# Cross-attention: other places for three kinds of transposes within an item, and two more scores ahead of the stage

## The chip, the cores and the metric

The kernel runs on one core of a Trainium2 chip. The metric is the device time of one execution in microseconds (us). The engines are named as in the profile: PE is TensorE, PEld its weight loads, DVE VectorE, ACT ScalarE, POOL GpSimd; SP issues most of the transfers.

## The reference

One decoder layer over x of 4 x 512 x 512, float32, in three parts, each added to x:

```
x = x + self_attention(layernorm(x))          # 16 heads of 128, causal, grouped keys
x = x + cross_attention(layernorm(x), ctx)    # 32 query heads of 16, 8 key heads of 16
x = x + ffn(layernorm(x))                     # 8 experts of 352, two for each token, one shared of 704

# cross-attention: q = layernorm(x), k = v = ctx (4 x 512 x 128), no projections
scores  = einsum('bkgsd,bktd->bkgst', qh, kh) / sqrt(16)
weights = softmax(scores)
out     = einsum('bkgst,bktd->bkgsd', weights, vh)
```

The change lies in the cross-attention.

## The kernel before, in words

The program is written engine by engine. Each engine runs its own instruction list in order, and waits on counters (semaphores) of the others. The three parts of the layer follow one another; the cross-attention lies between about 876 and 1265 us of the span.

**Items and steps.** The cross-attention is cut into 32 items (`ITEMS`): batch `m // 8` and key head `m % 8` of item `m`, with four query heads each. An item has 16 scores of 128x512 for the row maxima (`score`, line 1188), 16 transposed scores (line 1308) that ACT exponentiates (line 1560), and the product of the exponentials with the values (the results, line 1318). `cross_steps(m)` writes the order: eight steps `k` of 0 to 7, and in each: a score, two transposed scores, a score, perhaps a turn, and in the odd steps a quarter of the results of the item before (four matmuls of 32 columns side by side, one for each query head). PE, DVE and ACT all walk this one list, each taking the operations that are its own.

**The two kinds of scores.** A score goes to one of three PSUM banks, and DVE takes its row maximum out (`maximum`, line 1767); so the score `u` waits for the maximum of `u - 3`. The maxima of an item are subtracted inside the transposed scores, as two more rows of the queries (50 rows instead of 48). They must therefore be known before the item begins. So the scores run ahead of the items: `S_FIRST` of them are made in the tail of the self-attention (`START_CHAINS`, `START_END`, `START_MID`), and within item `m` the list makes scores `S_FIRST + 16 m` and following. A transposed score also has three banks, emptied by ACT's exponential.

**The turns.** A turn is a transpose on PE through one shared PSUM bank, `XT`. There are three kinds in an item, placed by `turns_in(m, k)`:

- the maxima turn `("m", m + 1)`: POOL splits the 16 maxima into a high and a low part (lines 996, 999), PE turns them (one matmul, line 196), ACT copies them out (line 1512), and SP moves them to DRAM and back into the rows of the queries (lines 780, 784);
- the raw turn: normalized queries `("q", ...)` in most even items, or the keys of a coming batch `("k", ...)` in items 1, 9 and 17: four matmuls, a copy of ACT (line 1516), a split by POOL (lines 947, 949), and transfers by SP (lines 736 to 772);
- the result turn `("o", m - 2)`: four matmuls that turn the results of item `m - 2`, which ACT copied out of PSUM at the end of item `m - 1` (line 1566). DVE then takes a reciprocal (line 1924) and at once divides (line 1906), and POOL adds to `res` (line 1007). Within DVE's list the reciprocal and the division stand behind the two maxima of the same step.

Each turn waits until the turn before it has been taken out of `XT`.

**Other work of DVE.** `norm_piece(b, kv, k)` puts the layer norms of the next batches at the ends of steps: the statistics of one tile (line 207), a group of small operations, or one normalized query tile (line 1752). Which items have one, and in which step, hangs on `m % 8` and the batch.

Of the kernel before, what the change touches and what calls it, by code (L numbers as in the profile page):

```python
# [68 lines left out]

FIRST_TURNS = [("k", 0), ("q", 0), ("q", 1), ("m", 0)]  # L70

S_FIRST = 30

START_CHAINS = {(2, 6): [("moments",)], (2, 8): [("roots",)], (3, 1): [("queries",)]}
START_END = {(3, 1): [("first_t", "k", 0)], (3, 2): [("first_t", "q", 0)], (3, 4): [("first_t", "q", 1)],
             (3, 14): [("first_t", "m", 0)]}
for at, us in ((6, (0, 1)), (7, (2, 3)), (8, (4, 5)), (10, (10, 11)), (11, (12, 13)), (12, (14, 15)), (18, (24, 25)),
               (19, (26, 27)), (20, (28, 29))):
    START_END[3, at] = [("first_s", u) for u in us]
for at, us in ((9, (6, 7)), (13, (16, 17)), (17, (20, 21))):  # L80
    START_CHAINS[3, at] = [("first_s", u) for u in us]
# [150 lines left out]
KV, XG, XD = 8, 4, 16  # L232
# [7 lines left out]
ITEMS = BATCH * KV  # L240
S_UNITS = XG * TOK_TILES
VW = 32


def turns_in(m, k):

    if k == 2 and m + 1 < ITEMS:
        return [("m", m + 1)]
    if k == 4 and m % 2 == 0 and m + 4 < ITEMS:
        return [("q", m // 2 + 2)]  # L250
    if k == 4 and m % KV == 1 and m + KV < ITEMS:
        return [("k", m // KV + 1)]
    if k == 6 and m >= 2:
        return [("o", m - 2)]
    return []


def cross_steps(m):


    ops = []
    for k in range(8):
        at = S_FIRST + S_UNITS * m + 2 * k
        units = [("s", n) for n in (at, at + 1) if n < S_UNITS * ITEMS]
        ops += units[0:1]
        if m < ITEMS:

            ops += [("st", 2 * k + 1), ("st", 2 * k)]
        ops += units[1:]
        ops += [("t",) + turn for turn in turns_in(m, k)]  # L270
        if 1 <= m <= ITEMS and k % 2:
            ops.append(("pv", k // 2))
        ops.append(("end", k))
    return ops

# [137 lines left out]
def mixed_tile(n):  # L413

    return n // 4 * 2 + n % 2, n // 2 % 2
# [8 lines left out]
def build(nc, x, ctx_in, w_qkv_t, w_proj_t, gate_t, w1_t, w2_t, w3_t, kinds, out):  # L424
# [11 lines left out]
    with ExitStack() as whole:  # L436
# [271 lines left out]
        def _(sp):  # L708
# [38 lines left out]
            def keep_queries(a):  # L747
                if a >= 2:
                    for n in (2 * a - 4, 2 * a - 3):
                        sp.wait_ge(s_xq3[n % 4], 32 * (n // 4 + 1))  # L750
                to_rows(q_way[a % 2], q_hi, q_lo, s_xqh, s_xql, a + 1, s_xqs)
# [100 lines left out]
            for m in range(ITEMS):  # L852
                if m + 1 < ITEMS:
                    move_maxima(m + 1)
                if m + 3 < ITEMS:
                    take_queries(m + 3)
                if m % KV == KV // 2 and m + KV < ITEMS:
                    take_keys(m // KV + 1, 0)
                if m % KV == 0 and m:
                    take_keys(m // KV, 1)  # L860
                for kind, n in turns_in(m, 4):
                    if kind == "q":
                        keep_queries(n)
                    else:
                        keep_keys(n)
                        if n + 1 < BATCH:
                            context(n + 1)
                for q in (2 * (m - KV - 1), 2 * (m - KV - 1) + 1):
                    if 0 <= q < N_ROUTED:
                        blank(q)  # L870
                if m >= ITEMS - 2:
                    load_piece(m - (ITEMS - 2), 0)
# [44 lines left out]
        def _(pool):  # L917
# [100 lines left out]
            def cross(m):  # L1018
# [11 lines left out]
                    clear_values(1)  # L1030
                if kv == 0 and b + 1 < BATCH:
                    order_keys(b + 1)
                for kind, n in turns_in(m, 4):
                    if kind == "q":
                        split_queries(n)
                    else:
                        split_keys(n)
                        build_values(n)
# [8 lines left out]
            for m in range(ITEMS + 2):  # L1047
                cross(m)
# [37 lines left out]
            for n in range(TOP * TILES):  # L1086
                t, r = mixed_tile(n)
# [8 lines left out]
        def _(pe):  # L1096
# [181 lines left out]
            def cross(m):  # L1278
                for op in cross_steps(m):
# [16 lines left out]
                    elif op[0] == "s":  # L1296
                        u = op[1]
                        pe.wait_ge(s_xmax, max(S_FIRST, u - 2))
                        score(u, XS + u % 3)
# [847 lines left out]
```

## Time and profile before

| | |
|---|---|
| time, median of 3 runs | 1773.65 us (1769.39 to 1777.32) |
| the profiled execution: own time | 1780.01 us |
| its span (first to last instruction) | 1778.1 us |
| mean granted clock of TensorE | 0.967 |
| PE busy | 1700.2 us, 96% of the span |
| DVE busy | 1213.6 us, 68% |
| ACT busy | 921.6 us, 52% |
| POOL busy | 182.8 us, 10% |

The busy shares are means over the three parts of the layer. The self-attention and the last part keep PE near full; in the cross-attention DVE has 16 maxima of 128x512 in each item beside its other work, and PE, DVE and ACT hand PSUM banks to one another every few hundred nanoseconds. A busy PE isn't PE at its peak, since matmuls overlap and their ends are modelled. What is read from a row below is thus the start of an instruction and the idle time before it.

### The profile page before, as it was taken

Reading aid. Unit: us, or ns where it says so; the run is one execution under the profiler, and the core shown is the slowest. Engines: PE = TensorE matmul, PEld = TensorE weight load, DVE = VectorE, ACT = ScalarE, POOL = GpSimd, SP = SyncE. Lnnn points to the kernel's source line nnn. Section 1 sums busy time; section 2 is a strip of 40 time slices with the busy share of each in tenths; the row PEclk is TensorE's granted clock in tenths of the full one; section 3 lists DMA queues with packets and bytes.
Section 4 is the critical chain, followed back from the end, with each engine's and each line's share of the span. In section 5 each row is a group of like instructions: output and inputs, shape, how many; then the busy total and the mean of one; then the engine's idle time right before and its main releaser. Section 6 shows DMA issues by size and latency. Waiting matters only on the chain.

```text
span 1778.1 us, 26288 instructions
## 1 busy us (share of the span) xinstructions
PE 1700.2 (96%) x9497; PEld 1303.7 (73%) x9497; DVE 1213.6 (68%) x2733; ACT 921.6 (52%) x1937; POOL 182.8 (10%) x297
## 2 busy tenths in 40 slices
PE   5799999999999999989899999999899999999998
PEld 4688888888888888876533333333699999999997
DVE  6666666666666666676589999997434267676766
ACT  2444445445444444442378887877431146666641
POOL 1000000000000000011122323221105100000024
PEclk9899999999999999997699999999799999999999
DMA  4000100010000000004023544442103178787846
GB/s 154 1 1 7 30 1 25 1 36 1 25 1 15 23 24 1 1 20 110 28 72 92 151 140 156 129 131 81 59 1 137 66 264 285 271 298 266 297 134 229
DMA packets 103203, 167.20 MB, mean 94 GB/s; under 512 B 8324, under 2 KB 52356, under 8 KB 102308
## 3 DMA queue, kind: packets, MB, share of 16 engines
q1 hardware_dynamic: 97956, 148.74, 25.9%
q0 software_dynamic: 5120, 16.78, 2.8%
q8 instruction: 77, 1.26, 0.3%
q14 instruction: 50, 0.41, 0.1%
HBM read 116.15 MB, written 49.28 MB: 93 GB/s over the span
## 4 chain that ended last, share of the span: by engine, by line
PE 84%; DVE 11%; ACT 3%; issue 1%; DMA 1%; POOL 0%; SPq 0%; DVEq 0%; ACTq 0%
PE ps L190 44%; PE ps L196 9%; PE ps L1433 8%; PE ps L1236 7%; PE ps L1318 6%; PE ps L1188 6%; DVE xmax L1767 4%; PE ps L1308 3%; DVE al L1782 1%; ACT ah L1538 1%; DVE stats L207 1%; PE ps L1369 1%; DVE ptl L1774 1%; DVE probs L1733 1%; ACT xp L1560 1%
## 5 line engine op out<-in xcount | busy, mean ns | idle before, releaser
L1767 DVE TENSOR_REDUCE xmax<-ps 128x1 f32<-128x512 f32 x512 | 319.1, 681 | 24.4 <-PE ps L1188 24.3
L1560 ACT ACTIVATE xp<-ps 128x512 f32<-128x512 f32 x512 | 273.5, 601 | 96.0 <-PE ps L1308 95.6
L1493 ACT ACTIVATE probs<-probs,nmax 128x128 f32<-128x128 f32 (+3 forms) x256 | 144.1, 563 | 160.7 <-DVE nmax L1733 160.7
L1188 PE MATMUL ps<-k,q 48*128 48x512 f32 x512 | 212.1, 487 | 8.0 <-DVE xmax L1767 5.1
L1308 PE MATMUL ps<-q,k 50*128 50x512 f32 x512 | 198.8, 472 | 6.1 <-ACT xp L1560 6.0
L1188 PEld LDWEIGHTS ps<-k,q 48*128 48x128 f32 x512 | 87.7, 192 | 147.4 <-DVE xmax L1767 113.0
L1533 ACT CAST pth<-ps 128x128 fp32r<-128x128 f32 (+3 forms) x256 | 107.0, 418 | 85.9 <-PE ps L196 85.9
L1318 PE MATMUL ps<-xp,vx 128*32 128x512 f32 x1024 | 140.1, 621 | 0.8 <-issue 0.8
L1733 DVE CUSTOM_DVE_ANT_0 probs<-ps,mask 128x128 f32<-128x128 f32 (+3 forms) x256 | 123.4, 482 | 10.0 <-PE ps L190 9.8
L1774 DVE TENSOR_TENSOR ptl<-ps,pth 128x128 fp32r<-128x128 f32 (+3 forms) x256 | 123.8, 484 | 2.0 <-ACT pth L1533 2.0
L196 PE MATMUL ps<-ident,probs 128*128 128x128 f32 x640 | 113.1, 275 | 8.7 <-DVE ptl L1774 6.6
L190 PE MATMUL ps<-w12h,x_h 128*128 128x352 f32 x568 | 121.1, 335 | 0.0
L1782 DVE TENSOR_TENSOR al<-ps,ah 128x512 fp32r<-128x512 f32 x64 | 44.2, 691 | 107.1 <-ACT ah L1538 107.1
L190 PE MATMUL ps<-w12h,x_l 128*128 128x352 f32 x568 | 116.0, 327 | 0.0
L190 PE MATMUL ps<-w12l,x_h 128*128 128x352 f32 x568 | 115.6, 326 | 0.0
L190 PE MATMUL ps<-xh,wh 128*128 128x512 f32 x384 | 111.7, 414 | 2.1 <-DVE wl L1711 2.1
L1949 DVE TENSOR_TENSOR w12l<-w_raw,w12h 128x1408 fp32r<-128x1408 f32 x56 | 90.7, 1620 | 27.9 <-ACT w12h L1591 27.9
L1308 PEld LDWEIGHTS ps<-q,k 50*128 50x128 f32 x512 | 81.8, 191 | 33.4 <-ACT xp L1560 26.7
L1742 DVE TENSOR_SCALAR probs<-probs,rinv 128x128 f32<-128x128 f32 (+3 forms) x256 | 99.8, 390 | 9.1
L1538 ACT CAST ah<-ps 128x512 fp32r<-128x512 f32 x64 | 37.6, 587 | 131.5 <-PE ps L1236 131.5
L196 PEld LDWEIGHTS ps<-ident,probs 128*128 128x128 f32 x640 | 81.7, 141 | 32.4 <-DVE probs L1742 10.3
L190 PE MATMUL ps<-xh,wl 128*128 128x512 f32 x384 | 105.3, 396 | 0.0
(188 smaller groups left out, 3553.6 us busy)
## 6 DMA issues: line engine op xcount, KB each, us to landing
w_raw<-in_w_t SPq DMA_DIRECT2D x56, 704.0 KB, 5.9
w_raw<-in_w_t SPq DMA_DIRECT2D x28, 768.0 KB, 5.8
q<-q_way SPq DMA_DIRECT2D x64, 192.0 KB, 3.2
rows_x<-w_raw SPq DMA_DIRECT2D x39, 256.0 KB, 3.4
mixed<-rows_x SPq DMA_DIRECT2D x39, 256.0 KB, 4.4
rows_y<-y_s SPq DMA_DIRECT2D x39, 256.0 KB, 5.4
q_way<-q_hi SPq DMA_DIRECT2D x32, 256.0 KB, 3.6
w_raw<-in_w_qkv_t SPq DMA_DIRECT2D x24, 256.0 KB, 3.0
```

The lines of the kernel that those rows point to most:

```text
L190: last = pe.matmul(dst, lhs, rhs, start=(n == 0), stop=(n == len(pairs) - 1))
L196: return pe.matmul(dst, src, ident, start=True, stop=True, is_transpose=True)
L1188: pe.matmul(ps[:, bank, :], q3[rows, m % 4, h // 2, i * P:(i + 1) * P].bitcast(F32R), k3[rows, m % KV, :].bitcast(F32R), start=True, stop= ...
L1236: pv = pe.matmul(ps[:, O_BANK + h % 2, j * P:], v[:, b % 2, j, :], p[:, 4 * j:3 * j + TOK_TILES, :].rearrange("p i n -> p (i n)"), start=( ...
L1308: pe.matmul(ps[:, XST + n % 3, :], k3[rows, m % KV, t * P:(t + 1) * P].bitcast(F32R), q3[rows, m % 4, h // 2, :].bitcast(F32R), start=True ...
L1318: ins = pe.matmul(ps[VW * h:VW * (h + 1), XO, :], vx[:, n // KV % 2, n % KV, j, :], xp[:, n % 2, h, j, :], start=(j == 0), stop=(j == TOK_ ...
L1433: ins = pe.matmul(ps[:, HY + n % 2, :], lhs, rhs, start=(step.opens and m == 0), stop=(step.closes and m == len(pairs) - 1))
L1493: act.activation(probs[u % 4][:, 0:w], probs[u % 4][:, 0:w], ACT.Exp, scale=-1.0, bias=nmax[:, u % 4:u % 4 + 1], accum_out=rsum[:, u % 4:u ...
L1560: act.activation(xp[:, m % 2, h, t, :], ps[:, XST + n % 3, :], ACT.Exp, scale=X_SCALE).then_inc(s_xe, 1)
L1733: dve.tensor_tensor_reduce(probs[u % 4][:, 0:w], ps[:, S_BANK + u % 2, 0:w], mask[:, SEQ - w:], -1.0, LARGEST, ALU.add, ALU.min, nmax[:, u ...
L1767: dve.tensor_reduce(xmax[:, m % 2, h % 2, h // 2, i:i + 1], ps[:, bank, :], AX_X, ALU.max, negate=True).then_inc(s_xmax, 1)
L1774: dve.tensor_tensor(ptl[:, i:4 * i + 1:3, :], ps[:, T_BANK + (1 + t) % 2, 0:(i + 1) * P].rearrange("p (j n) -> p j n", n=P), pth[:, i:4 * ...
```

## The change

`MAXIMA_AT, RAW_AT, RESULT_AT = 1, 5, 7` takes the place of the steps 2, 4 and 6 of the three kinds of turns. In these odd steps a quarter of the results follows as well: the raw turn and the result turn stand ahead of it, the maxima turn behind it. DVE's reciprocal and division move with the result turn, from the end of step 6 to the end of step 7. `S_FIRST` grows from 30 to 32: scores 30 and 31 go to the last step of the self-attention, and every item makes scores that are two further ahead. SP's and POOL's lists read `RAW_AT` where they read 4 before; their own order is unchanged.

```diff
-S_FIRST = 30
+S_FIRST = 32
...
-               (19, (26, 27)), (20, (28, 29))):
+               (19, (26, 27)), (20, (28, 29, 30, 31))):
...
+MAXIMA_AT, RAW_AT, RESULT_AT = 1, 5, 7
+
+
 def turns_in(m, k):
 
-    if k == 2 and m + 1 < ITEMS:
+    if k == MAXIMA_AT and m + 1 < ITEMS:
         return [("m", m + 1)]
-    if k == 4 and m % 2 == 0 and m + 4 < ITEMS:
+    if k == RAW_AT and m % 2 == 0 and m + 4 < ITEMS:
         return [("q", m // 2 + 2)]
-    if k == 4 and m % KV == 1 and m + KV < ITEMS:
+    if k == RAW_AT and m % KV == 1 and m + KV < ITEMS:
         return [("k", m // KV + 1)]
-    if k == 6 and m >= 2:
+    if k == RESULT_AT and m >= 2:
         return [("o", m - 2)]
...
-        ops += [("t",) + turn for turn in turns_in(m, k)]
+        ops += [("t",) + turn for turn in turns_in(m, k) if k != MAXIMA_AT]
         if 1 <= m <= ITEMS and k % 2:
             ops.append(("pv", k // 2))
+        ops += [("t",) + turn for turn in turns_in(m, k) if k == MAXIMA_AT]
```

**PE's list, the maxima turn.** L1188 (L1192 in the change) is a score for a maximum, L1308 (L1312) a transposed score, L1318 (L1322) a quarter of the results, `xm` the split maxima. Before, from step 1 of an item on:

```order
L1188 MATMUL ps<-k,q 128x512
L1318 MATMUL ps<-xp,vx 32x512 x4
L1188 MATMUL ps<-k,q 128x512
L1308 MATMUL ps<-q,k 128x512 x2
L1188 MATMUL ps<-k,q 128x512
L196 MATMUL ps<-ident,xm 32x128
```

Now, from the same place on:

```order
L1192 MATMUL ps<-k,q 128x512
L1322 MATMUL ps<-xp,vx 32x512 x4
L196 MATMUL ps<-ident,xm 32x128
L1192 MATMUL ps<-k,q 128x512
L1312 MATMUL ps<-q,k 128x512 x2
```

The turn of the maxima now stands between the results and the next score, where nothing stood.

**PE's list, the raw turn and the result turn of an even item.** `xn` are the normalized queries, `o_t` the results of item `m - 2`. Before, from step 4 on; the last quarter of the results follows the last row:

```order
L196 MATMUL ps<-ident,xn 128x128 x4
L1188 MATMUL ps<-k,q 128x512
L1308 MATMUL ps<-q,k 128x512 x2
L1188 MATMUL ps<-k,q 128x512
L1318 MATMUL ps<-xp,vx 32x512 x4
L1188 MATMUL ps<-k,q 128x512
L1308 MATMUL ps<-q,k 128x512 x2
L1188 MATMUL ps<-k,q 128x512
L196 MATMUL ps<-ident,o_t 128x128 x4
L1188 MATMUL ps<-k,q 128x512
L1308 MATMUL ps<-q,k 128x512 x2
L1188 MATMUL ps<-k,q 128x512
```

Now, from step 5 on:

```order
L196 MATMUL ps<-ident,xn 128x128 x4
L1322 MATMUL ps<-xp,vx 32x512 x4
L1192 MATMUL ps<-k,q 128x512
L1312 MATMUL ps<-q,k 128x512 x2
L1192 MATMUL ps<-k,q 128x512 x2
L1312 MATMUL ps<-q,k 128x512 x2
L1192 MATMUL ps<-k,q 128x512
L196 MATMUL ps<-ident,o_t 128x128 x4
L1322 MATMUL ps<-xp,vx 32x512 x4
L1192 MATMUL ps<-k,q 128x512
```

Both turns now stand between the last score of an odd step and its results; before, each had two scores and two transposed scores between itself and the next results.

**DVE's list, the reciprocal and the division.** L1767 (L1771) is a maximum, L207 a layer norm's statistics of one tile. Before, from the last maxima ahead of step 4 of an item on:

```order
L207 BN_STATS stats<-res 128x6
L1767 TENSOR_REDUCE xmax<-ps 128x1 x6
L1924 RECIPROCAL xrec<-ps 128x16
L1906 TENSOR_TENSOR xo<-ps,xrec 128x256
L1767 TENSOR_REDUCE xmax<-ps 128x1 x10
```

Now:

```order
L207 BN_STATS stats<-res 128x6
L1771 TENSOR_REDUCE xmax<-ps 128x1 x8
L1928 RECIPROCAL xrec<-ps 128x16
L1910 TENSOR_TENSOR xo<-ps,xrec 128x256
L1771 TENSOR_REDUCE xmax<-ps 128x1 x8
```

The division stands behind all 16 maxima of the item, where it stood ahead of the last two.

## Rows read from the trace of the kernel before

**Rows 1.** Groups of instructions, 930 to 1180 us: busy us, mean ns | idle before it.
```profile
L1767 DVE TENSOR_REDUCE xmax<-ps 128x1 f32<-128x512 f32 x348 | 216.1, 681 | 11.7 <-PE ps L1188 11.7
```

**Rows 2.** Windows of 50 us, busy us by engine, granted clock, DMA share, GB/s.
```profile
930.00:980.00 50.00, 49.32 (x311) 19.17 (x310) 47.89 (x84) 40.41 (x82) 11.03 (x18) 1.00 0.31 83
```

**Rows 3.** Timeline of DVE, item 6: start us, us, instructions [idle before <-releaser].
```profile
953.12 2.48 DVE L1767 TENSOR_REDUCE xmax<-ps 128x1 f32<-128x512 f32 x4 [0.22 <-PE ps L1188]
955.52 0.68 DVE L207 BATCH_NORM_STATS2 stats<-res 128x6 f32<-128x512 f32 x1
956.12 2.47 DVE L1767 TENSOR_REDUCE xmax<-ps 128x1 f32<-128x512 f32 x4
958.81 1.29 DVE L1767 TENSOR_REDUCE xmax<-ps 128x1 f32<-128x512 f32 x2 [0.22 <-PE ps L1188]
960.01 0.25 DVE L1924 RECIPROCAL xrec<-ps 128x16 f32<-128x16 f32 x1
...
960.64 3.67 DVE L1767 TENSOR_REDUCE xmax<-ps 128x1 f32<-128x512 f32 x6
```

**Rows 4.** Timeline of PE, item 6.
```profile
951.16 0.50 PE L1188 MATMUL ps<-k,q 48*128 48x512 f32 x1
...
951.59 1.06 PE L1318 MATMUL ps<-xp,vx 128*32 128x512 f32 x8
...
952.58 0.50 PE L1188 MATMUL ps<-k,q 48*128 48x512 f32 x1
...
953.25 0.28 PE L196 MATMUL ps<-ident,xm 128*32 128x128 f32 x1
...
953.47 0.49 PE L1188 MATMUL ps<-k,q 48*128 48x512 f32 x1
...
953.86 0.49 PE L1188 MATMUL ps<-k,q 48*128 48x512 f32 x1
...
955.94 0.66 PE L196 MATMUL ps<-ident,xn 128*128 128x128 f32 x4
...
956.53 0.50 PE L1188 MATMUL ps<-k,q 48*128 48x512 f32 x1
```

**Rows 5.** Timeline of DVE, item 22: an even item without statistics.
```profile
1138.45 2.48 DVE L1767 TENSOR_REDUCE xmax<-ps 128x1 f32<-128x512 f32 x4 [0.21 <-PE ps L1188]
1141.14 2.54 DVE L1767 TENSOR_REDUCE xmax<-ps 128x1 f32<-128x512 f32 x4 [0.21 <-PE ps L1188]
1144.07 1.29 DVE L1767 TENSOR_REDUCE xmax<-ps 128x1 f32<-128x512 f32 x2 [0.39 <-PE ps L1188]
```

**Rows 6.** Timeline of DVE, item 26: statistics in every odd step.
```profile
1184.14 2.47 DVE L1767 TENSOR_REDUCE xmax<-ps 128x1 f32<-128x512 f32 x4
1186.52 0.68 DVE L207 BATCH_NORM_STATS2 stats<-res 128x6 f32<-128x512 f32 x1
```

**Rows 7.** Timeline of PE, the last results of the stage: a result turn ahead of results.
```profile
1259.96 0.66 PE L196 MATMUL ps<-ident,o_t 128*128 128x128 f32 x4
...
1260.55 1.07 PE L1318 MATMUL ps<-xp,vx 128*32 128x512 f32 x8
```

**Rows 8.** Timeline, the start of the cross-attention.
```profile
874.54 1.28 DVE L1767 TENSOR_REDUCE xmax<-ps 128x1 f32<-128x512 f32 x2
...
875.97 0.47 PE L1188 MATMUL ps<-k,q 48*128 48x512 f32 x1 [1.64 <-DVE xmax L1767]
...
876.47 2.48 DVE L1767 TENSOR_REDUCE xmax<-ps 128x1 f32<-128x512 f32 x4 [0.65 <-PE ps L1188]
```

**Rows 9.** Timeline of PE, item 30, which has next to no scores.
```profile
1239.67 0.66 PE L196 MATMUL ps<-ident,o_t 128*128 128x128 f32 x4
...
1240.86 1.06 PE L1318 MATMUL ps<-xp,vx 128*32 128x512 f32 x8
```

**Rows 10.** Window of 2 us in item 1, columns as in rows 2.
```profile
894.00:896.00 2.00, 2.00 (x12) 0.26 (x10) 1.50 (x3) 1.25 (x4) 0.00 (x0) 0.50 0.03 8
```

**Rows 11.** DMA issues: KB each, us to landing.
```profile
q<-q_way SPq DMA_DIRECT2D x64, 192.0 KB, 3.2
```

More of the change, by code:

```diff
@@ L860, in _ @@
                     take_keys(m // KV, 1)
-                for kind, n in turns_in(m, 4):
+                for kind, n in turns_in(m, RAW_AT):
                     if kind == "q":
@@ L1032, in cross @@
                     order_keys(b + 1)
-                for kind, n in turns_in(m, 4):
+                for kind, n in turns_in(m, RAW_AT):
                     if kind == "q":
```

## The prediction

> **What bounds the kernel now.** I read the groups of instructions first, then the windows, and then the timelines of DVE and PE over one item, since the change touches the cross-attention alone. There 348 maxima take DVE 216.1 us of a stretch of 250 us, and the only idle time ahead of them is 11.7 us, all of it waiting for a score from PE [rows 1]. The window shows both engines close to full, DVE 47.89 and PE 49.32 of 50 us, at a granted clock of 1.00, which is the level of 2.4 GHz [rows 2]. 348 maxima are 21.75 items, so an item takes 11.5 us. The stage runs at DVE's pace plus what PE makes it wait, with a few tenths of slack on either engine in each item. The order inside an item decides who waits.
>
> Where does DVE wait? Four maxima on end take 2.40 us, 0.60 each: 953.12 to 955.52. The next four, from 956.12 to 958.81, take 2.69 [rows 3]. So 0.29 us are lost there, and the row says PE. I rebuild that loss from PE's starts, since all that follows is made in the same way. Call the start of the first score of an even step 0. Its maximum begins at 0.54 (952.58 to 953.12) [rows 3, 4] and ends 0.68 later [rows 1], at 1.22. That frees the bank for the last score of the odd step, which starts at 1.28 (952.58 to 953.86). Its results follow 0.43 later (951.16 to 951.59) and hold PE for 0.99 (951.59 to 952.58) [rows 4]. So the next step's first score starts at 2.70, and its maximum can start at 3.24. DVE, with four maxima, is free at 0.54 + 2.40 = 2.94. The difference, 0.30, is the 0.29 of the row. **Every odd step thus has a window that PE overruns by 0.29 us, unless DVE has other work in it.** Where it has, nothing is lost: with a tile's statistics between the maxima the next four follow without idle time [rows 3, 6]. The reciprocal and the division, 0.63 together (960.01 to 960.64) [rows 3], stand after the 14th maximum and lie in the window of step 7: the six maxima behind them run on without a stop.
>
> **The change, part by part.** No operation is added or removed. Four things move. At full clock there are items 2 to 29; they have a window at each odd step.
>
> *Raw turn, step 4 to step 5.* Four transposes hold PE for 0.59 (955.94 to 956.53) [rows 4]. In an even step they cost little: where no statistics stand ahead, the window of step 5 loses 0.53 instead of 0.29 (1141.14 to 1144.07 is 2.93) [rows 5]. Where statistics do, it loses the plain 0.29 of rows 3. Now the turn stands between the last score and the results: 1.28 + 0.43 + 0.59 + 0.99 + 0.54 = 3.83 against 2.94, a loss of 0.89. Items 4, 6, 12 and 14 have statistics in step 3: 4 x 0.60. Eight other even items and the two key turns of items 9 and 17: 10 x 0.36. Item 26 has statistics in step 5 too, of 0.60: 0.29. Sum **6.3 us**.
>
> *Result turn, step 6 to step 7.* It holds PE for the same 0.59, and nothing hides under results that follow: at the stage's end the results start 0.59 after such a turn (1259.96 to 1260.55) [rows 7]. The window of step 7 is then 3.83 on PE. On DVE it keeps the division, now behind its last maximum: 2.94 + 0.63 = 3.57. The loss is 0.26 where it was none. It goes where DVE has a query tile or statistics in that window as well (items 2, 10, 18, 26, 27, 28); 22 items are left: **5.7 us**.
>
> *Maxima turn, step 2 to behind the results of step 1.* It holds PE for 0.22 (953.25 to 953.47) [rows 4]. In step 2 that was hidden, since an even step has time to spare. Now it makes the window of step 1 lose 0.51 instead of 0.29, in the 13 items where DVE has no layer norm work at the ends of steps 0 and 1 (5 to 8, 13 to 16, 21 to 25): **2.9 us**. It could cost 0 (it hides) or 0.33 (with 0.11 us of lead that PE loses to the later result turn); I take the turn's own row. Its consumers gain: the maxima go out to DRAM and back a step earlier.
>
> On the maxima turn the Trainium skill has a rule that would make it cheaper. TensorE: Matmul & The Clock Gate, section "Part 3: Packing small matmuls", says that matmuls on different column strips of the array run at the same time. The turn has 32 columns, as each of the four results matmuls does, so by that rule it would run beside the last of them and the 2.9 us would be about 0.
>
> *Two more scores ahead.* Before, PE waits 1.64 us at the stage's start for maximum 29, and DVE then 0.65 for score 30 (876.47) [rows 8]. Now score 30 goes as soon as maximum 28 is out, at 874.54 + 0.68 = 875.22; maxima 30 and 31 follow at about 875.8 and 876.4; score 32 waits for all 32, until 877.1, and its maximum comes at 877.6. Before, it came at 876.47 + 2 x 0.60 = 877.67. DVE gains nothing; the gap moves. But the items begin 1.1 us later, and item 30 has one more step without scores to do after the last maximum: **1.2 us** lost.
>
> *The end.* Items 30 and 31 have next to no scores, and PE and ACT wait for one another there. In item 30 the result turn has two transposed scores between itself and the results (1239.67 to 1240.86) [rows 9], so ACT has work while PE turns. In step 7 it stands straight ahead of the results: 0.59, plus 0.22 for the item's maxima turn: **0.8 us**. For item 31 I count nothing; its bound is the same 0.6. Item 1 runs at half clock as well (0.50, 1.2 GHz) [rows 10]; PE is busy for all of that row while DVE has 1.50 of 2.00, so a turn costs the same wherever it stands: I take **0.3 us** for the maxima turn.
>
> Sum: 6.3 + 5.7 + 2.9 + 1.2 + 0.8 + 0.3 = **17.2 us** slower. The profiled execution took 1780.0 and would take 1797.2; it stands 6.4 above the median of the runs, 1773.65. I forecast from that median: **1791 us**. The lower bound of the sum has every turn hidden: 10 x 0.24 of today's raw turns are won, 1.2 is lost at the start, -1.2 in all. The upper has each turn pay in full and DVE's other work cover nothing: 14 x 0.6 + 22 x 0.59 + 13 x 0.33 + 2.3 = 28.
>
> **The rivals.**
>
> 1. *Covered turns* (not slower). PE catches up within each window because its 0.43 between score and results is slack, and the turns fit there or run beside the results. Place: steps 1, 5 and 7. Price: the lower bound, 1772.5 us. It decides if the loop's extra cost is under 0.25 us an item (28 x 0.25 = 7, plus the 2.3 of start and end, is the half per cent). For it: two matmuls of different row halves do overlap on PE. Against it: the turn ahead of results in rows 7 and the 0.24 that today's raw turn costs even an even step [rows 5]. Chance 0.14.
> 2. *The maxima turn alone is hidden*, by the rule above: 17.2 - 2.9 gives 1788 us. No row of before has this turn beside results, so neither side is shown. Chance 0.12.
> 3. *The clock.* In item 1 the granted clock is 0.50, and DVE is busy for 75% of the row [rows 10] instead of 96% [rows 2]: an item of 11.5 us becomes one of 14.7. What PE does ahead of that stretch changes a little with the two scores. If the stretch lasts an item longer it costs 3.2 us more, 1794; if it stays away, as much less, 1788. Chance 0.10 together.
> 4. *Late queries.* The raw turn, POOL's split and the transfers come a step later, 11.5 / 8 = 1.4 us. The queries taken in item `m` are used from item `m + 1` on, and land 3.2 us after their issue [rows 11], against 5 us and more that are left. If they came late, a step in each even item: 13 x 1.4 more, 1809. Chance 0.03.
> 5. *As forecast*, 1791 us: chance 0.61.
>
> That the lists don't change as said is out: the rows of the two orders show the moves.
>
> **How the numbers follow.** Half a per cent, 8.9 us, is about what a measurement of this kernel can tell from no change. Cases 2 to 5 lie above that, save where their sums are half of what I made them; case 1 lies within it. Faster by over half a per cent needs covered turns and a shorter stretch of low clock and luck on top: 0.05. Within: 0.16. Slower: 0.79. The range leaves out the lower part of case 1 and case 4: 1778 to 1802.
>
> **What would show it.** In DVE's timeline of an even item without statistics, four maxima of step 4 and 5 should end in an idle time of about 0.8 us, and the division should be followed by about 0.2 us of idle time where there was none. The idle time ahead of the maxima from 930 to 1180 us should grow from 11.7 to about 23 us (22 items by 14.9 / 28 more), all of it put down to scores, and an item should grow from 11.5 us to about 12.0 in the mean. Idle times that stay at 0.22 would make the window wrong; an unchanged step 1 the maxima turn; a wait on a transfer or on POOL ahead of a turn would mean another mechanism.

## The result, and the profile after

The changed kernel takes **1796.77 us** (median of 4 runs, 1790.61 to 1801.21) against 1773.53 (4 runs, 1769.39 to 1777.32): a ratio of **1.0122**, with a 95% interval of 1.009 to 1.0153, or 16 to 27 us. It is slower, as forecast; the forecast of 1791 lies 6 us below the median and in the range. The profiled execution of the changed kernel took 1801.21 us, with a span of 1799.3 and a granted clock of 0.968. Its lines are those of before plus 4.

The groups of instructions, 930 to 1180 us, answer to [rows 1]:

```profile
L1771 DVE TENSOR_REDUCE xmax<-ps 128x1 f32<-128x512 f32 x327 | 203.0, 682 | 23.9 <-PE ps L1192 23.9
```

The forecast for this idle time was about 23 us. In the same 250 us there are 327 maxima where 348 were: an item takes 250 / (327 / 16) = 12.2 us instead of 11.5. That is more than the forecast of about 12.0; DVE's other work in the stretch is 1.2 us longer as well. DVE's timeline of item 22, an even item without statistics, answers to [rows 5]:

```profile
1151.84 2.48 DVE L1771 TENSOR_REDUCE xmax<-ps 128x1 f32<-128x512 f32 x4 [0.25 <-PE ps L1192]
1154.76 2.48 DVE L1771 TENSOR_REDUCE xmax<-ps 128x1 f32<-128x512 f32 x4 [0.43 <-PE ps L1192]
1157.45 2.48 DVE L1771 TENSOR_REDUCE xmax<-ps 128x1 f32<-128x512 f32 x4 [0.21 <-PE ps L1192]
1160.73 2.48 DVE L1771 TENSOR_REDUCE xmax<-ps 128x1 f32<-128x512 f32 x4 [0.80 <-PE ps L1192]
1163.13 0.25 DVE L1928 RECIPROCAL xrec<-ps 128x16 f32<-128x16 f32 x1
1163.41 0.42 DVE L1910 TENSOR_TENSOR xo<-ps,xrec 128x256 f32<-128x256 f32 x1
1164.09 2.49 DVE L1771 TENSOR_REDUCE xmax<-ps 128x1 f32<-128x512 f32 x4 [0.25 <-PE ps L1192]
```

Each stop is where the windows put it. Four maxima take 2.40 us; what a start lies further behind is lost, unless DVE has other work there. Window of step 1, with the maxima turn: 1154.76 - 1151.84 - 2.40 = 0.52 (forecast 0.51). Step 3, unchanged: 0.29 (0.29). Step 5, with the raw turn: 0.88 (0.89). Step 7: 0.96, of which the reciprocal and the division are 0.63 [rows 3]; that leaves 0.33, where 0.26 was forecast and none was lost before.

PE's timeline shows the maxima turn, which now stands straight behind results, and the raw turn and the result turn, which stand straight ahead of them:

```profile
1153.01 1.06 PE L1322 MATMUL ps<-xp,vx 128*32 128x512 f32 x8
1154.01 0.28 PE L196 MATMUL ps<-ident,xm 128*32 128x128 f32 x1
1154.22 0.50 PE L1192 MATMUL ps<-k,q 48*128 48x512 f32 x1
...
1158.62 0.66 PE L196 MATMUL ps<-ident,xn 128*128 128x128 f32 x4
1159.20 1.06 PE L1322 MATMUL ps<-xp,vx 128*32 128x512 f32 x8
1160.20 0.49 PE L1192 MATMUL ps<-k,q 48*128 48x512 f32 x1
...
1161.91 0.66 PE L196 MATMUL ps<-ident,o_t 128*128 128x128 f32 x4
1162.49 1.06 PE L1322 MATMUL ps<-xp,vx 128*32 128x512 f32 x8
1163.49 0.50 PE L1192 MATMUL ps<-k,q 48*128 48x512 f32 x1
```

No turn is hidden beside results: the maxima turn holds PE for 0.21 us behind them (1154.01 to 1154.22), the raw turn and the result turn for 0.58 each ahead of them. In step 7 PE takes 3.29 us from score to score (1160.20 to 1163.49), as forecast (3.83 less the 0.54 of a hand-over). What is longer is the hand-over: the maximum behind the division starts 0.60 us behind its score (1163.49 to 1164.09), where the others start 0.53 to 0.54 behind theirs. The waits of PE from 930 to 1180 us went from 2.2 us for ACT's exponentials to 18.6, in 71 pieces of up to 0.3. Before and now:

```profile
PE ps L1308 <- ACT xp L1560: 2.2, 9, 0.3
```

```profile
PE ps L1312 <- ACT xp L1564: 18.6, 71, 0.3
```

These look like a new bound, but the windows gave three of the four stops to 0.01 us without them, and every stop of DVE is put down to a score.

**Window by window.** The same can be read for every odd step of items 2 to 28: the time from the first maximum of one even step to the first maximum of the next, in the changed kernel less that of the kernel before (its second profile, experiment 5). Summed by step, in us, with the kernels of experiment 1, which have the two scores ahead and move one turn alone:

| window of | forecast | changed | maxima turn alone | raw turn alone | result turn alone |
|---|---|---|---|---|---|
| step 1 | 2.9 | 3.1 | 2.7 | 0.1 | 0.0 |
| step 3 | 0 | 0.0 | 0.1 | 0.0 | 0.1 |
| step 5 | 6.3 | 6.3 | 0.0 | 6.3 | 0.0 |
| step 7 | 5.7 | 8.3 | 0.8 | 1.5 | 8.3 |

Steps 1 and 5 grow in the items that the prediction named and by its amounts: 13 items by 0.21 to 0.24 us, items 4, 6, 12 and 14 by 0.59, ten by 0.35 to 0.38, item 26 by 0.29. Step 7 grows by 0.33 in most items. In each kernel with one turn moved, 0.3 us of step 7 stand at the end of item 12, which every kernel with 32 scores ahead has, and 0.4 to 1.0 us are a late transfer (experiment 1).

In the changed kernel step 7 has a second price, which the sum didn't have: in items 2, 10 and 18 no score is late, but DVE's query tile takes 1.05 to 1.07 us instead of 0.77. POOL's second split of the queries now runs beside it:

```profile
1013.32 1.28 POOL L953 TENSOR_TENSOR q_lo<-q_raw,q_hi 128x512 fp32r<-128x512 f32 x1
```

```profile
1014.05 1.05 DVE L1756 TENSOR_SCALAR xn<-res,mv,rstd 128x512 f32<-128x512 f32 x1
```

By these rows 0.55 us of the tile lie beside the split, and it ends 0.50 us behind it. That comes to 0.9 us in the three items.

**By part of the stage.** The loop is counted from the first maximum of the stage (maximum 28) to the end of the last, the end from there to the last reciprocal, the rest from there to the end of the span. The rows for these marks, first the end before, then the changed kernel's, which answer to [rows 8] and to the end of the stage:

```profile
1230.77 2.47 DVE L1767 TENSOR_REDUCE xmax<-ps 128x1 f32<-128x512 f32 x4
...
1263.08 0.26 DVE L1924 RECIPROCAL xrec<-ps 128x16 f32<-128x16 f32 x1 [1.70 <-PE ps L196]
```

```profile
874.89 2.56 DVE L1771 TENSOR_REDUCE xmax<-ps 128x1 f32<-128x512 f32 x4
...
1247.81 2.48 DVE L1771 TENSOR_REDUCE xmax<-ps 128x1 f32<-128x512 f32 x4 [0.22 <-PE ps L1192]
...
1286.76 0.26 DVE L1928 RECIPROCAL xrec<-ps 128x16 f32<-128x16 f32 x1 [1.70 <-PE ps L196]
```

| profile | loop | end | rest |
|---|---|---|---|
| before | 358.7 | 29.8 | 515.0 |
| before, a second profile (experiment 5) | 358.1 | 25.8 | 511.6 |
| changed | 375.4 | 36.5 | 512.5 |

The loop is 17.0 us longer than the mean of the two before (forecast 15.2), the end 6.6 or 10.7 (forecast 2.0), depending on which profile of before one takes. The rest runs the same code in all kernels and varies by a few us from execution to execution, so a few us between two profiles mean little unless they are traced to a row.

In the end the clock fell. Windows of the changed kernel, columns as in [rows 2]:

```profile
1254.00:1260.00 6.00, 4.64 (x26) 1.41 (x25) 0.00 (x0) 4.92 (x10) 0.00 (x0) 0.99 0.53 138
1260.00:1263.00 3.00, 3.00 (x13) 1.02 (x13) 1.17 (x4) 1.27 (x3) 0.45 (x1) 0.50 1.06 393
1264.00:1270.00 6.00, 4.53 (x26) 1.36 (x25) 0.00 (x0) 4.93 (x11) 0.00 (x0) 1.00 0.00 0
1271.00:1283.00 12.00, 10.99 (x48) 2.86 (x40) 0.68 (x2) 2.99 (x6) 0.73 (x1) 0.50 0.01 1
```

Twice PE is busy for only 4.64 and 4.53 of 6 us, since it waits for ACT at each pair of steps, and twice the granted clock then drops to 0.50, the level of 1.2 GHz: for 3 us and for 12.

### The profile page after: what moved, and what is told of

Read it like the earlier page. It is cut to its first block, busy times and chain, and to the rows that moved or that the text cites. A ratio compares the mean times of both kernels' runs of the same rounds, so it can differ in the third digit from the quotient of the medians.

```text
span 1799.3 us, 26292 instructions
## 1 busy us (share of the span) xinstructions
PE 1701.0 (95%) x9497; PEld 1304.4 (72%) x9497; DVE 1216.4 (68%) x2733; ACT 921.9 (51%) x1937; POOL 179.5 (10%) x297
## 4 chain that ended last, share of the span: by engine, by line
PE 82%; DVE 10%; ACT 6%; issue 1%; DMA 0%; POOL 0%; DVEq 0%; ACTq 0%
PE ps L190 44%; PE ps L196 9%; PE ps L1437 8%; PE ps L1240 7%; PE ps L1322 6%; PE ps L1192 4%; PE ps L1312 3%; DVE xmax L1771 3%; ACT xp L1564 3%; DVE al L1786 1%; ACT ah L1542 1%; PE ps L1373 1%; DVE stats L207 1%; DVE ptl L1778 1%; ACT o_t L1570 1%
## 5 line engine op out<-in xcount | busy, mean ns | idle before, releaser
L1771 DVE TENSOR_REDUCE xmax<-ps 128x1 f32<-128x512 f32 x512 | 318.5, 682 | 39.5 <-PE ps L1192 39.4
L1564 ACT ACTIVATE xp<-ps 128x512 f32<-128x512 f32 x512 | 265.0, 605 | 76.2 <-PE ps L1312 75.8
L1312 PE MATMUL ps<-q,k 50*128 50x512 f32 x512 | 193.5, 464 | 29.5 <-ACT xp L1564 28.9
L1192 PE MATMUL ps<-k,q 48*128 48x512 f32 x512 | 199.8, 475 | 4.7 <-DVE xmax L1771 3.0
L1192 PEld LDWEIGHTS ps<-k,q 48*128 48x128 f32 x512 | 88.4, 193 | 108.8 <-DVE xmax L1771 92.5
L1312 PEld LDWEIGHTS ps<-q,k 50*128 50x128 f32 x512 | 85.8, 191 | 88.3 <-ACT xp L1564 85.1
L1322 PE MATMUL ps<-xp,vx 128*32 128x512 f32 x1024 | 142.8, 633 | 0.7 <-issue 0.7
```

Of the source, the lines that this page charges most:

```text
L1192: pe.matmul(ps[:, bank, :], q3[rows, m % 4, h // 2, i * P:(i + 1) * P].bitcast(F32R), k3[rows, m % KV, :].bitcast(F32R), start=True, stop= ...
L1312: pe.matmul(ps[:, XST + n % 3, :], k3[rows, m % KV, t * P:(t + 1) * P].bitcast(F32R), q3[rows, m % 4, h // 2, :].bitcast(F32R), start=True ...
L1322: ins = pe.matmul(ps[VW * h:VW * (h + 1), XO, :], vx[:, n // KV % 2, n % KV, j, :], xp[:, n % 2, h, j, :], start=(j == 0), stop=(j == TOK_ ...
L1564: act.activation(xp[:, m % 2, h, t, :], ps[:, XST + n % 3, :], ACT.Exp, scale=X_SCALE).then_inc(s_xe, 1)
L1771: dve.tensor_reduce(xmax[:, m % 2, h % 2, h // 2, i:i + 1], ps[:, bank, :], AX_X, ALU.max, negate=True).then_inc(s_xmax, 1)
```

## Experiments

**1. One part at a time.** Four kernels keep the two scores ahead and put the turns at other places; the changed kernel has `1, 5, 7`.

```diff
-MAXIMA_AT, RAW_AT, RESULT_AT = 1, 5, 7
+MAXIMA_AT, RAW_AT, RESULT_AT = 2, 4, 6
```

> Only the two more scores ahead; the three turns stand at steps 2, 4 and 6 as before. Windows theory: the loop keeps its idle times (0.22 us in plain odd steps, 0.39 after a raw turn, none in step 7), about 0.54 us of idle time of DVE an item, and the whole is 1 to 2 us slower than before (one more step without scores in item 30). Rival, that the two scores ahead cause the longer end of the changed kernel (36.5 instead of 29.8 us from the last maximum to the last reciprocal): 5 us or more slower than before, with the longer end in the trace.

```diff
+MAXIMA_AT, RAW_AT, RESULT_AT = 1, 4, 6
```

> The two more scores ahead and the maxima turn behind the results of step 1; raw and result turns at steps 4 and 6. Windows theory: step 1 idles 0.44 us instead of 0.22 in the items without layer norm work there, 13 times 0.22 = 2.9 us over the kernel with the two scores ahead alone; the other windows stay. Rival, that the turn hides beside the results: no difference to that kernel, step 1 at 0.22.

```diff
+MAXIMA_AT, RAW_AT, RESULT_AT = 2, 5, 6
```

> The two more scores ahead and the raw turn at step 5 ahead of the results; the others at steps 2 and 6. Windows theory: 0.80 us idle in step 5 of even items and of items 9 and 17, 6.3 us over the kernel with the two scores ahead alone; odd items unchanged. Rival, that the result turn's division behind the last maximum is what costs: no more than 1 us here.

```diff
+MAXIMA_AT, RAW_AT, RESULT_AT = 2, 4, 7
```

> The two more scores ahead and the result turn with its division at step 7; the others at steps 2 and 4. Windows theory: 0.25 us idle behind the division in 22 items, and steps 5 of even items as before (0.39): 5.7 us in the loop and 0.6 at the end over the kernel with the two scores ahead alone. Rival, that only turns without DVE work beside them cost: 0 to 1 us here.

| kernel | time | ratio to before (95%) | less scores ahead alone | loop | end | idle 930 to 1180 |
|---|---|---|---|---|---|---|
| scores ahead alone | 1776.42 | 1.0023 (1.0004 to 1.0041) | | 366.0 | 27.0 | 16.0 |
| and maxima turn | 1779.33 | 1.0036 (1.0015 to 1.0057) | 2.9 | 361.5 | 28.5 | 14.5 |
| and raw turn | 1782.32 | 1.0066 (1.0042 to 1.0090) | 5.9 | 366.1 | 26.9 | 18.6 |
| and result turn | 1787.47 | 1.0074 (1.0046 to 1.0103) | 11.1 | 368.4 | 36.3 | 17.1 |

The median of before in these runs is 1772.2. The intervals of the four ratios are 3 to 5 us on either side. The medians give 2.9 us for the maxima turn (2.9 forecast) and 5.9 for the raw turn (6.3); taken from the ratios the three differences would be 2.3, 7.6 and 9.0. So the agreement to a tenth is luck, and the sizes are read from the windows: by the table above the maxima turn makes its stop in step 1, the raw turn in step 5, the result turn in step 7, and none at another turn's place. Two rows of item 22, with the maxima turn alone and with the result turn alone:

```profile
1142.30 2.48 DVE L1771 TENSOR_REDUCE xmax<-ps 128x1 f32<-128x512 f32 x4 [0.43 <-PE ps L1192]
```

```profile
1152.64 2.48 DVE L1771 TENSOR_REDUCE xmax<-ps 128x1 f32<-128x512 f32 x4 [0.38 <-PE ps L1192]
...
1155.99 2.49 DVE L1771 TENSOR_REDUCE xmax<-ps 128x1 f32<-128x512 f32 x4 [0.24 <-PE ps L1192]
```

Two don't. The result turn costs 11.1 instead of 5.7 and 0.8, and its end is as long as the changed kernel's, 36.3 us. And the two scores ahead alone cost 4.2 instead of 1.2, with a loop that is 7.6 us longer. Of these, 2.2 us are item 1, which took 16.6 us instead of 14.4, at half clock for longer. Where most of the rest comes from PE's timeline of that kernel shows:

```profile
1137.67 0.46 PE L1192 MATMUL ps<-k,q 48*128 48x512 f32 x1 [1.13 <-DMA q<-q_way]
```

```profile
1134.00:1140.00 6.00, 4.66 (x32) 1.90 (x32) 4.83 (x9) 4.46 (x9) 1.16 (x3) 0.97 0.48 156
1140.00:1146.00 6.00, 6.00 (x27) 1.71 (x21) 3.31 (x6) 2.66 (x6) 0.00 (x0) 0.50 0.03 8
```

A score two units further ahead needs its queries a step earlier, and at the start of item 22 they had not landed: PE waits 1.13 us, and the granted clock then stands at 0.50 through the next 6 us, in which DVE is busy for 3.31 us (before, in the same 6 us: 5.37). The changed kernel has no wait for a transfer anywhere in its loop.

**2. Is it chance?** The same kernel, profiled a second time.

> The kernel with only the two scores ahead (turns at 2, 4, 6), a second profile. If the late queries of the first profile (1.1 us of wait for the transfer at 1137 us, and half clock behind it) belong to the two scores ahead, a wait of 0.5 us or more for the same tile stands in the middle of the loop again, and the idle before the maxima from 930 to 1180 us is 14 us or more. If they came by chance, there is none, and the idle is 11 to 12.5 us, as before.

```profile
1137.23 0.46 PE L1192 MATMUL ps<-k,q 48*128 48x512 f32 x1 [1.51 <-DMA q<-q_way]
```

The wait stands at the same place again, 1.51 us of 3.0 in all, and the idle time from 930 to 1180 us is 14.5. This time the clock did not fall, and the loop takes 362.0: 3.6 longer than before's 358.4 (mean of two), of which 3.0 are these waits. The end is 27.0 and 26.9 in the two profiles, 1.2 longer than the 25.8 of before's second profile (experiment 5): that is the 1.2 of the forecast. The fall of the clock behind the wait is chance. Late queries as such are not the two scores' alone. Before's own first profile has one such wait, at the start of item 26, and its second has none:

```profile
1181.76 0.47 PE L1188 MATMUL ps<-k,q 48*128 48x512 f32 x1 [1.00 <-DMA q<-q_way]
```

The layout of before with cut columns (experiment 7), with 30 ahead as well, has 1.2 us in three waits. What the two scores do is to make them longer or more frequent in a loop of before's pace: 1.9 and 3.0 us in the two profiles, 0.4 to 1.0 in the three kernels that move a turn besides.

**3. 30 scores ahead, with the new turns.**

```diff
-S_FIRST = 32
+S_FIRST = 30
-               (19, (26, 27)), (20, (28, 29, 30, 31))):
+               (19, (26, 27)), (20, (28, 29))):
```

> The changed kernel with 30 scores ahead instead of 32 (turns at 1, 5, 7). The two more scores ahead are what cost 4 us alone (1776.4 against 1772.2): then this gives 3 to 5 us back, 1791 to 1794. That is the theory if GpSimd has the maxima ready for the turn behind the results of step 1, which in the kernel before it had some 0.3 us ahead of that place. Rival: the maxima are late at this place, TensorE waits for them at most items, 0.3 to 1.0 us of it each, and the time is 1800 to 1820. Second rival: the 4 us belonged to a late transfer of queries in a kernel that ran its loop faster (1.1 us of wait and some 4 us at half clock behind it), which the slower loop here doesn't meet: no change, 1795 to 1798.

1788.34 us, a ratio of 1.0076 (1.0051 to 1.0101). The loop takes 375.6, as in the changed kernel (375.4): in sum the two more scores ahead neither cost nor save anything there. GpSimd's maxima are late for three turns, 0.7 us in all, so the rival by which they come late in most items falls. In the profiles the difference sits in the end, 27.2 us at full clock against 36.5. The time came out under all three expectations, since none had thought of the end. The stop of step 7 in item 22 is now the forecast's:

```profile
1157.56 2.48 DVE L1771 TENSOR_REDUCE xmax<-ps 128x1 f32<-128x512 f32 x4 [0.81 <-PE ps L1192]
...
1160.85 2.48 DVE L1771 TENSOR_REDUCE xmax<-ps 128x1 f32<-128x512 f32 x4 [0.18 <-PE ps L1192]
```

1160.85 - 1157.56 - 2.40 - 0.63 = 0.26. So the 0.07 on top belongs to the 32 scores ahead. In the code one more wait (`s_ml`) stands ahead of the first maximum of each item's 16, and only with 32 ahead is that the maximum at this stop; that this wait is the 0.07 wasn't tried by itself.

**4. The end alone.** The result turn goes back to step 6, but only in items 30 to 33.

```diff
-    if k == RESULT_AT and m >= 2:
+    if k == (RESULT_AT if m < ITEMS - 2 else 6) and m >= 2:
```

> The changed kernel, but in items 30 to 33, and there alone, the result turn stands at step 6 again. Theory: the long end (36.5 us from the last maximum to the last reciprocal, 29.8 before) comes from the result turn straight ahead of the results in the items that have no scores left, where TensorE then idles and falls to half clock: the end goes to 28 to 31 us and the time to 1790 to 1793. Rival: the end is long because of the two scores ahead or by how the clock happens to fall: the end stays at 35 us or more and the time at 1796 to 1798.

1791.83 us, a ratio of 1.0106 (1.0076 to 1.0137). The loop is the same to 0.01 us (375.41), the end 28.1 instead of 36.5. PE's timelines of item 30 show what the place does. In the changed kernel:

```profile
1259.86 0.75 PE L1312 MATMUL ps<-q,k 50*128 50x512 f32 x1 [0.45 <-ACT xp L1564]
1260.54 1.12 PE L196 MATMUL ps<-ident,o_t 128*128 128x128 f32 x4
1261.58 1.92 PE L1322 MATMUL ps<-xp,vx 128*32 128x512 f32 x8
```

With the turn at step 6, and the window of 6 us around it:

```profile
1257.07 0.50 PE L1312 MATMUL ps<-q,k 50*128 50x512 f32 x2
1257.50 0.66 PE L196 MATMUL ps<-ident,o_t 128*128 128x128 f32 x4
1258.08 0.67 PE L1312 MATMUL ps<-q,k 50*128 50x512 f32 x2
1258.68 1.06 PE L1322 MATMUL ps<-xp,vx 128*32 128x512 f32 x8
```

```profile
1254.00:1260.00 6.00, 5.55 (x38) 2.04 (x31) 1.64 (x5) 4.82 (x10) 0.74 (x1) 1.00 0.79 234
```

At step 6 the four transposes fill the 0.45 us in which PE would wait for ACT. At step 7 the wait stays and the turn comes on top, and PE is idle at every pair of steps of the item. In the one profile PE was busy for 5.55 of the 6 us and the clock stayed at 1.00, in the other for 4.64 and it fell. That a fall must follow isn't shown: with 30 ahead the turn stood at step 7 too, and the clock stayed. Nor is a fall seen behind every stretch of so little work: in the 6 us that follow in this kernel PE is busy for 4.71 us, in the 6 us around the late queries of experiment 2 for 4.28, and both were granted the full clock:

```profile
1260.00:1266.00 6.00, 4.71 (x27) 1.27 (x24) 0.18 (x2) 4.92 (x10) 0.00 (x0) 1.00 0.38 140
```

```profile
1134.00:1140.00 6.00, 4.28 (x31) 1.50 (x30) 4.54 (x9) 4.12 (x8) 1.17 (x3) 1.00 0.52 153
```

And the times of the two kernels, 1.0106 and 1.0122, are not told apart by their intervals.

**5. Before, a second profile.** The kernel before itself, since its first profile has a fallen clock in the end too.

> The kernel before itself, a second profile, to see which part of its end belongs to it. In its first profile the end (last maximum to last reciprocal) took 29.8 us, 10 of them at a granted clock of 0.50; the changed kernel took 36.5 with 16 at half clock. If the fall is part of this order of work, it stands here again and the end is 29 to 31 us. If it came by chance in that execution, the end is 26 to 28 us at full clock, as with the two scores ahead alone (26.9 in two profiles), and the changed kernel's end costs 9 to 10 us and not 6.6. The loop in front of it should repeat in either case: idle before the maxima 930 to 1180 us of 11.5 to 12 us.

The loop repeats (358.1, idle time 11.8). The end doesn't: 25.8 us, with a clock of 1.00 up to the last reciprocal. So 4 us of the end in the profile that the prediction was made from were chance, and measured against full clock the changed kernel's end cost 10.7 us in the execution that was profiled, not 6.6.

**6. Shorter windows, by heads.** If the windows are the mechanism, taking half of the results out of an odd step should take the stops away. First, two of the four heads were moved behind the scores of the next even step (step 7 stays whole), in both layouts.

```diff
-        if 1 <= m <= ITEMS and k % 2:
-            ops.append(("pv", k // 2))
+        if 1 <= m <= ITEMS:
+            ops += [("pv",) + part for part in PV_AT[k]]
...
+PV_AT = {0: [], 1: [(0, (0, 1))], 2: [(0, (2, 3))], 3: [(1, (0, 1))], 4: [(1, (2, 3))], 5: [(2, (0, 1))],
+         6: [(2, (2, 3))], 7: [(3, (0, 1, 2, 3))]}
```

> The layout of before (turns at 2, 4, 6, 30 scores ahead), but the eight result matmuls of an odd step are cut in two: two heads stay at the odd step, two go behind the scores of the next even step; the last product (step 7) stays whole. The work is the same. Theory, the window: a score can go in only three maxima after the one before the last, 3 x 0.60 = 1.8 us, and VectorE idles where TensorE's own work between two scores (results 1.00, a turn 0.28 or 0.59, two scores 0.33 each, some 0.3 of handing over) is longer. Halved results take 0.5 out of every odd window, so the idle of 0.22 in odd steps goes; the raw turn then shares step 4 with half of the results, which leaves some 0.25 in half of the items. Idle before the maxima from 930 to 1180 us: from 11.7 to 2 to 6 us; time 1760 to 1767, below both kernels. Rival, the handing over: idle is the price of passing the turn's bank round and not of the work in the window; then idle stays near 11 us and the time near 1772.

> The changed kernel (turns at 1, 5, 7, 32 ahead) with the results halved in the same way. The window: at step 1 half of the results and the maxima turn fit (0.44 goes to 0), at step 5 half of the results and the raw turn leave some 0.25 of the 0.80, at step 7 the results are whole and the turn still costs 0.25. Idle from 930 to 1180 us: from 23.9 to 7 to 11 us; time 1774 to 1783, 14 to 22 us less than the changed kernel. The handing over: nothing changes by more than in the kernel with the old layout, so it stays at 1787 or more and some 23 us above that one.

1835.56 and 1835.89 us: 61 us slower, and the layout of the turns makes no difference any more. PE's timeline of the first:

```profile
1151.38 1.06 PE L1322 MATMUL ps<-xp,vx 128*32 128x512 f32 x8
1152.37 0.50 PE L1192 MATMUL ps<-k,q 48*128 48x512 f32 x1
...
1156.06 1.05 PE L1322 MATMUL ps<-xp,vx 128*32 128x512 f32 x4
1157.04 0.50 PE L1192 MATMUL ps<-k,q 48*128 48x512 f32 x1
```

Two heads (4 records) hold PE for 0.98 us, four heads (8 records) for 0.99. They run side by side, so half of them is no less time. The expectation's half was wrong, and the kernel says nothing on the windows: from 930 to 1180 us PE is busy for 48.7 us and more of each 50, and DVE waits for it for 43 us, wherever the turns stand. That matmuls on different column strips of the array run at the same time is what the Trainium skill states (TensorE: Matmul & The Clock Gate, "Part 3: Packing small matmuls"), and these rows agree. The turn of 32 columns gains nothing by it: behind the results it holds PE for 0.21 us, in step 2 for 0.22 [rows 4]. The four results take all four strips (`tile_position=(0, VW * h)` for the four heads `h`), so none is left free beside them.

**7. Shorter windows, by columns.** All four heads, but 256 of the 512 columns at the odd step and 256 at the next even one; steps 3 and 5 only.

```diff
+PV_AT = {0: [], 1: [(0, 0, 512)], 2: [], 3: [(1, 0, 256)], 4: [(1, 256, 512)], 5: [(2, 0, 256)], 6: [(2, 256, 512)],
+         7: [(3, 0, 512)]}
...
-                            ins = pe.matmul(ps[VW * h:VW * (h + 1), XO, :], vx[:, n // KV % 2, n % KV, j, :],
-                                            xp[:, n % 2, h, j, :], start=(j == 0), stop=(j == TOK_TILES - 1),
+                            ins = pe.matmul(ps[VW * h:VW * (h + 1), XO, cols], vx[:, n // KV % 2, n % KV, j, :],
+                                            xp[:, n % 2, h, j, cols], start=(j == 0), stop=(j == TOK_TILES - 1),
```

> The layout of before, and the results of steps 3 and 5 cut in two by columns: 256 of the 512 columns of all four heads at the odd step, the other 256 behind the scores of the next even step; steps 1 and 7 stay whole. (Cut by heads it had cost 61 us, since two heads took the 1.05 us that four take.) The window: if 256 columns take half of the time, 0.5 to 0.55 us, the odd windows 3 and 5 lose their 0.22 and 0.39; the raw turn shares step 4 with half of the results, which leaves at most 0.25 there. Idle before the maxima from 930 to 1180 us: from 11.7 to 3 to 8 us; time 1762 to 1771. The handing over (idle is the price of passing the turn's bank on): idle stays at 11 to 12, time 1772 to 1777. If a cut costs time of its own, the eight records take more than 0.6 us and the time rises.

> The changed kernel with the same cut. The window: step 5 keeps some 0.27 of its 0.80 in even items and none of its 0.22 in odd ones, step 3 none; steps 1 (0.44) and 7 (0.25) are as they were. Idle from 930 to 1180 us: from 23.9 to 14 to 18 us; time 10 to 16 us under the changed kernel, 1781 to 1787. The handing over: the turns of steps 5 and 7 cost what they did, idle 23 to 24, time 1795 to 1800.

The layout of before: 1774.27 us, 1.0015 (0.9996 to 1.0034). The changed layout: 1782.91 us, 1.0065 (1.0049 to 1.0081), 14 us under the changed kernel; the layouts differ by 8.6 us instead of 23.2, though not all of that is the loop, as shown below. The second's timeline of item 22:

```profile
1149.67 4.87 DVE L1776 TENSOR_REDUCE xmax<-ps 128x1 f32<-128x512 f32 x8 [0.44 <-PE ps L1196]
1155.00 2.53 DVE L1776 TENSOR_REDUCE xmax<-ps 128x1 f32<-128x512 f32 x4 [0.46 <-PE ps L1196]
...
1158.56 2.48 DVE L1776 TENSOR_REDUCE xmax<-ps 128x1 f32<-128x512 f32 x4 [0.41 <-PE ps L1196]
```

Step 1, which was left whole, still loses 0.44. Step 3 loses nothing: eight maxima run on. Step 5 keeps 0.46 of 0.80. The turns are all still passed on through the same bank, so the price is not that of the passing; it is what stands in the window. Both idle times missed their expectations, 18.4 us instead of 14 to 18, and 13.5 instead of 3 to 8 in the layout of before, because the cut isn't free and fills the even steps. A half holds PE for 0.57 us, not 0.50 (1150.88 to 1151.45 in the first's timeline):

```profile
1150.88 0.64 PE L1323 MATMUL ps<-xp,vx 128*32 128x256 f32 x8
1151.45 0.50 PE L1192 MATMUL ps<-k,q 48*128 48x512 f32 x1
```

Step 7's idle time goes from 0.25 to 0.41, since step 6 ahead of it now has half of the results to do. In the layout of before the raw turn meets half of the results in step 4, and the idle time moves there. Over items 2 to 28 the cut takes 7.9 us out of the windows that end behind steps 3 and 5 there, and puts 8.4 into that of step 7, although no turn was moved. Its loop took 363.8 us in the profile, 5.4 more than before's; of these, 3.9 are item 1, at half clock for longer. Of what the changed layout gains by the cut, 6.4 us are loop in the profiles (369.0, with item 1 2.4 us longer) and 8.7 are the end (27.8 us, at full clock). No version beat the kernel before.

## Why the prediction was right, and where its sizes were off

- **Windows of the odd steps.** Right, to 0.01 us in three windows of item 22, and 0.07 short in the fourth; over items 2 to 28 the stops stand in the items that were named. The prediction's rows of before gave the length that PE needs between two scores; adding the turns gave the stops. The cut by columns shows that the window's content and not the passing of the bank is what is paid.
- **Raw turn, 6.3.** 6.3 by the windows, in the changed kernel and alone (5.9 by the medians of the times).
- **Maxima turn, 2.9.** 3.1 by the windows in the changed kernel and 2.7 alone (2.9 by the medians). The rival by which it hides beside the results is out: 0.21 us on PE behind them. By that rival it would run beside the last of the four; they run side by side themselves, over all the columns.
- **Result turn, 5.7.** The stop stands where it was forecast, but is 0.33 and not 0.26, alone as in the changed kernel (1152.64 to 1155.99 is 3.35, less 2.40 and 0.63). With 30 scores ahead it is 0.26, so the two scores and the turn add up to more than either alone. Step 7 is 8.3 us longer in all: 21 of the 22 named items have the stop (7.0 us; the 22nd, item 29, has no score left behind it), item 12 has 0.35 more, and the query tiles beside POOL's split are the other 0.9. Its kernel alone lost 11.1 us by the medians, since it has the long end too, and its loop of 10.0 us more than before's holds a late transfer (0.8) and item 1 at half clock for longer, 16.6 us instead of 14.4:

```profile
896.00:902.00 6.00, 6.00 (x28) 2.55 (x26) 2.58 (x4) 2.76 (x5) 2.90 (x5) 0.50 0.41 137
```

  In the changed kernel that stretch has 0.82 on the mean, before it had 0.85.
- **Loop, 15.2 in all.** 17.0. Step 7 alone is 2.6 longer than its forecast. Of the 0.3 for item 1 nothing came: it took 14.3 us, before 14.4. Rival 3, the clock in item 1, is there from profile to profile and not by layout: the item took 13.8 to 18.3 us in the twelve profiles without the cut by heads, and 16.6 and 13.8 in the two of one kernel (the scores ahead alone).
- **Two more scores ahead, 1.2.** The gain at the start is nothing and the end 1.2 longer, as forecast (26.9 against 25.8). What was missed is that the scores then need their queries a step earlier, and these come late: 1.9 and 3.0 us alone, where before had 1.0 and none, and more if the clock falls behind it. Rival 4 had late queries for another reason, the raw turn a step later. In the changed kernel, whose items are slower, the wait doesn't occur, so this doesn't touch the sum.
- **The end, 0.8 (and 1.2 of the scores ahead).** This is the **mis-sized term**: 2.0 forecast, 6.6 to 10.7 in the profiles. At full clock it is about right, 27.2 with 30 ahead and 27.8 with the columns cut, against 25.8. The other 9 us go with the 15 us at half clock, at a place where the forecast counted only the transposes' own time. I had looked for a change of the clock in item 1 alone (rival 3), and had taken the end of the profile of before for the rule, which a second profile shows to be 4 us too long. What makes it fall there stays open, and in how many executions of the changed kernel it does: in its one profile and in that of the result turn alone it did. Its runs go from 1790.61 to 1801.21, a spread of about that size, but the spread doesn't show it: with the result turn of the last items back at step 6 (experiment 4) they go from 1787.73 to 1799.27. In both kernels the longer runs are those with the lower mean clock (0.968 at 1801.21, 0.974 at 1790.61), and where in them it was low is not on record.

The sum of 17.2 put the forecast at 1791. The loop's 17.0 and an end of 2 to 11 give 1793 to 1801 from the same median; the four runs lie at 1790.61, 1793.07, 1800.47 and 1801.21. So the order of events in the loop is what the prediction had right. That the median lies well inside the range owes something to chance, since two of the four runs lie within 2 us of its upper end, and the sum has no term for what sets them apart from the other two.

## What to carry to other kernels

Where two engines pass a few buffers to one another, write down how long the one takes between two hand-overs and what the other has to do meanwhile; a piece of work costs nothing in a window that has room and its full length in one that doesn't, so its place decides and not its amount. A piece that fills a wait of the same engine also keeps that wait from adding up with others. Two changes that each look small can share a place: here the two scores ahead made the result turn's stop longer. Before a long stretch of a profile is taken as belonging to a kernel, a second profile is worth having, since a fall of the clock in it can be chance.

## What the runs showed that I had not expected

- PE need not stand still for the clock to fall. In the end of the changed kernel no wait ahead of a fall was over 0.57 us; PE was busy for 4.6 of 6 us, twice, and each time the granted clock went to 0.50 afterwards, and stayed there for 12 us the second time with PE busy for 10.99 of them. In the kernel with the scores ahead alone a single wait of 1.13 us had 6 us at 0.50 behind it, and a wait of 1.51 us in its second profile had none, with PE busy for 4.28 of the 6 us around it.
- Half of a group of side-by-side matmuls takes the time of the whole: 0.98 us for two heads, 0.99 for four. Cut by columns the half takes 0.57.
- DVE's query tile (128x512, tensor by scalar) takes longer beside POOL's split of the queries: 0.77 us without it, 1.05 to 1.07 with 0.55 us of the tile beside it, and 1.54 to 1.56 with 1.04 in the changed layout with cut columns. In each case it ends 0.5 us behind the split. The kernels that move all three turns have the two side by side; none of those with one turn moved has.
